# Twelve odd heads in rounded passes, their halves made during the attention

## What is computed

```python
x = x + attn(layernorm(x))        # elu(q)+1, elu(k)+1; kv = kp^T v; out = qp kv / (z + EPS)
x = x + xattn(ctx, ctx, layernorm(x), ssm_kernel, D, 8)
x = x + ffn(layernorm(x))         # 16 experts, top 4, and a shared expert

# xattn, for k = v = ctx (8, 256, 512), 32 heads of 8 channels, sequence 256:
kv = einsum('bhil,bhjl->bijhl', k_, v_)          # products of channel pairs
y = irfft(rfft(kv) * rfft(ssm_kernel))[..., :L]  # causal convolution for each head
out = einsum('bijhl,bhil->bjhl', y + kv * D, q_)
```

## Time and profile before

| | |
|---|---|
| median of 3 runs | 861.2 us (860.97 to 863.88) |
| the profiled execution | 860.96 us, span 859.1 us |
| TensorE busy | 840.3 us, 98% |
| DVE, ACT, POOL busy | 543.6, 378.1, 446.6 us |
| attention | 0 to about 243 us |
| heads 2 to 31 | 249 to 399 us |
| TensorE's granted clock, mean | 0.997 |

### The profile page before, as it was taken

How to read it: one execution, slowest core, us unless ns; L and a number is a source line. 1 busy time by engine, 2 the same in 40 slices (tenths; PEclk the granted TensorE clock), 3 DMA queues, 4 the chain that set the end, 5 groups by cost and what they waited for, 6 DMA issues and landing times.

```text
span 859.1 us, 14219 instructions
## 1 busy us (share of the span) xinstructions
PE 840.3 (98%) x4346; PEld 702.4 (82%) x4346; DVE 543.6 (63%) x849; ACT 378.1 (44%) x608; POOL 446.6 (52%) x439
## 2 busy tenths in 40 slices
PE   8999999999999999999999999999999999999995
PEld 7888888889877777778888778888888888888884
DVE  6767767775657777888769875544555544555431
ACT  5313322333133533442652255555555555655552
POOL 2123213331068899884622344666656666656644
PEclk9999999999999999999999999999999999999998
DMA  9611101100026543440210396988989888999866
GB/s 286 239 40 33 18 25 36 37 12 13 1 62 197 167 128 111 124 133 16 93 63 6 116 339 154 224 200 209 194 190 222 203 217 191 191 198 223 204 118 85
DMA packets 55108, 114.21 MB, mean 133 GB/s; under 512 B 10720, under 2 KB 14816, under 8 KB 54944
## 3 DMA queue, kind: packets, MB, share of 16 engines
q1 hardware_dynamic: 38048, 73.28, 27.3%
q0 software_dynamic: 17024, 40.48, 25.3%
HBM read 83.07 MB, written 30.67 MB: 132 GB/s over the span
## 4 chain that ended last, share of the span: by engine, by line
PE 88%; DVE 5%; issue 2%; POOL 1%; ACT 1%; DMA 1%; POOLq 0%; DVEq 0%; ACTq 0%
PE PS L206 20%; PE PS L208 20%; PE PS L207 19%; PE PS L217 17%; PE PS L1647 4%; PE PS L706 2%; PE PS L697 1%; PE PS L635 1%; PE PS L640 1%; PE PS L1584 1%; PE PS L1574 1%; PE PS L1614 1%; PE PS L1583 1%; PE PS L1566 1%; DMA QY<-stat_d 1%
## 5 line engine op out<-in xcount | busy, mean ns | idle before, releaser
L206 PE MATMUL PS<-QY_rounded,wh 128*128 128x512 f32 (+1 forms) x376 | 153.2, 407 | 0.0
L208 PE MATMUL PS<-QY_rounded,wl 128*128 128x512 f32 (+1 forms) x376 | 145.7, 387 | 0.0
L1362 POOL DMA_INDIRECT out_y<-QY,idy x72 | 114.5, 1590 | 44.9 <-ACT QY L1456 33.6
L207 PE MATMUL PS<-QY_rounded,wh 128*128 128x512 f32 (+1 forms) x312 | 120.0, 385 | 0.0
L1918 DVE TENSOR_TENSOR hTl<-hh,hTh 128x512 fp32r<-128x512 f32 (+1 forms) x39 | 27.5, 705 | 107.6 <-ACT hTh L1437 104.1
L1339 POOL DMA_INDIRECT xg<-xs_d,idx x64 | 76.8, 1200 | 28.8 <-issue 14.2
L208 PEld LDWEIGHTS PS<-QY_rounded,wl 128*128 128x128 f32 x376 | 70.6, 188 | 15.1
L217 PE MATMUL PS<-qER,Tz 128*128 128x288 f32 x320 | 81.1, 407 | 0.5 <-DVE QY L1064 0.4
L217 PE MATMUL PS<-prod,Tz 128*128 128x288 f32 x320 | 80.5, 406 | 0.2 <-DVE term L1047 0.2
L206 PEld LDWEIGHTS PS<-QY_rounded,wh 128*128 128x128 f32 x376 | 71.0, 189 | 11.1
L1456 ACT ACTIVATE QY<-PS,WPOS 128x512 f32<-128x512 f32 x76 | 52.4, 690 | 55.1 <-PE PS L208 45.2
(11 more groups left out here) (238 smaller groups left out, 1868.3 us busy)
## 6 DMA issues: line engine op xcount, KB each, us to landing
ws<-in_gu_w SPq DMA_DIRECT2D x38, 512.0 KB
ws<-in_dn_w SPq DMA_DIRECT2D x20, 512.0 KB, 5.6
C<-in_ctx SPq DMA_DIRECT2D x32, 256.0 KB, 2.7
Tz<-kpad_d SPq DMA_DIRECT2D x32, 256.0 KB, 3.3
xs_d<-xn SPq DMA_DIRECT2D x16, 256.0 KB, 2.0
out_y<-X SPq DMA_DIRECT2D x16, 256.0 KB
X<-in_x SPq DMA_DIRECT2D x1, 3072.0 KB, 17.5
xn<-in_xT SPq DMA_DIRECT2D x6, 512.0 KB, 3.4
```

What stands on the lines that cost most here:

```text
L206: pe.matmul(out_, lh, rh, start=first, stop=False)
L207: pe.matmul(out_, lh, rl, start=False, stop=False)
L208: return pe.matmul(out_, ll, rh, start=False, stop=last)
L1362: nc.gpsimd.indirect_dma_start(out=out, out_offset=bass.IndirectOffsetOnAxis(ap=idy[:, t:t + 1], axis=0), in_=yo[:, t], in_offset=None, co ...
```

## The change

Twelve odd heads (HALVES: 7, 9, ... 29) are convolved with three_pass, from halves of their products and of their Toeplitz rows. The Toeplitz halves are made once from kpad (POOL, into aTh and aTl) and stored in kpad_hl_d. The halves of the products are made during the attention, two heads in each of the batches 1 to 6: POOL makes the products into prod (in two parts and a small one), ACT rounds them into a free part of QY, POOL subtracts, and SP stores both to prod_hl_d. In the convolution stage SP loads them again, high and low part at different heads (load_half), into two sets of new buffers. The other twenty heads (WHOLE) stay as they were, but share the two product buffers in a new order, and the loops over heads are written out. mr, the spread statistics, moves from QY to Tz[0]. On DVE x_add comes before z_lo, att_norm(b) ends step b, and ln_norm(1, b-2) follows the next batch's statistics. Semaphores of the weight halves are merged into w_hi and w_lo; shared_lo comes in six parts in place of three.

```diff
+AHEAD = 2
+HALVES = [2 * m + 1 for m in range(3, 3 + AHEAD * (B - DIRECT))]
+WHOLE = [h for h in range(CH) if h not in HALVES]
...
+            def ahead_batch(b, last=False):
+                n = b * AHEAD - DIRECT * AHEAD
+                made = b * AHEAD_STEP - DIRECT * AHEAD_STEP
+                for j in range(AHEAD):
+                    sp.wait_ge(ahead_hi, n + (j + 1))
+                    store_half(0, n + j, ahead_high, hi_out)
+                    sp.wait_ge(ahead, made + AHEAD_MADE[j])
+                    if last:
+                        load_context(sp, WHOLE[j], j)
+                    else:
+                        ahead_context(n + AHEAD + j, j)
+                    sp.wait_ge(ahead, made + AHEAD_LOW[j])
+                    store_half(1, n + j, ahead_prod, lo_out)
...
+            def products_ahead(j, s):
+                pool.wait_ge(c2_in[j], s * 16 + 16)
+                wait_apart(pool, lo_out, s * (16 * AHEAD) + 16 * j)
...
+            def low_ahead(j, s):
+                wait_apart(pool, ahead_hi, s * AHEAD + j + 1)
+                nc.gpsimd.tensor_tensor(ahead_prod.bitcast(F32R), ahead_prod, ahead_high, ALU.subtract).then_inc(ahead, 1)
...
+            def high_ahead(b, j):
+                n = b - (DIRECT - 1)
+                wait_apart(act, ahead, n * AHEAD_STEP + AHEAD_MADE[j])
+                wait_apart(act, hi_out, n * (16 * AHEAD) + 16 * j)
+                act.activation(ahead_high.bitcast(F32R), ahead_prod, ACT.Copy).then_inc(ahead_hi, 1)
...
                 if not first:
+                    x_add(b - 1)
                     if not (last or isinstance(b, int) and b < DIRECT - 1):
                         z_lo(b + 1)
-                    x_add(b - 1)
                 kv_mask(b)
...
+                def load_half(n, j):
+                    k = n % 2
+                    if n < len(HALVES):
+                        t, dst = ((TzHi[k], odd_h[k]), (TzLo[k], odd_l[k]))[j]
+                        src = bass.AP(tensor=kpad_hl_d.tensor, offset=(j * CH + HALVES[n]) * (KPAD + 1), ap=[[1, P], [1, D]])
+                        sp.dma_start(t[:], src).then_inc(halves_in[k], 16)
+                        sp.dma_start(dst[:].rearrange("p c b n -> p (c b n)"), prod_hl_d[j, n]).then_inc(halves_in[k], 16)
...
+                def convolve_halves(h, behind=None):
+                    n, m = HALVES.index(h), h // 2
+                    k = n % 2
+                    pe.wait_ge(halves_in[k], 64 * (n // 2 + 1))
+                    pe.wait_ge(y_read[1], 2 * m)
+                    for c in range(DC):
+                        o = PS[:, DC + c].rearrange("p (b n) -> p b n", n=YGAP)[:, :, 0:NPAIR]
+                        for r in range(c + 1):
+                            w = slice((c - r) * P, (c - r + 1) * P)
+                            mm = three_pass(pe, o, TzHi[k][:, w].bitcast(F32R), TzLo[k][:, w].bitcast(F32R), odd_h[k][:, r].bitcast(F32R), odd_l[k][:, r].bitcast(F32R), r == 0, r == c)
```

More of the change, by code:

```diff
@@ L136, in decoder_program @@
         kpad_done, kpad_out = sem("kpad_done"), sem("kpad_out")
+        kpad_hl = [a[:].rearrange("p c s -> p (c s)")[0:CH, 0:KPAD + 1] for a in (aTh, aTl)]
+        ahead, ahead_hi = sem("ahead"), sem("ahead_hi")
+        hi_out, lo_out = sem("ahead_hi_out"), sem("ahead_lo_out")
+        halves_in = [sem(f"halves_in{k}") for k in range(2)]
+        NPROD = B * NPAIR
+        ahead_high = QY[:].rearrange("p c b s -> p c (b s)")[:, :, (B - 2) * S:(B - 2) * S + NPROD]
+        ahead_prod = prod[0][:].rearrange("p c b n -> p c (b n)")
+        AHEAD_MADE, AHEAD_LOW, AHEAD_STEP = (3, 7), (4, 8), 8
         tz_in = [sem(f"toeplitz_in{k}") for k in range(2)]
@@ L328, in _ @@
             pool.wait_ge(xns[1], TPB * B)
-            products(pool, 1, 0)
+            products(pool, 2)
         @block_.scalar
@@ L529, in step @@
             def step(b, first=False, last=False):
-                if not first:
-                    att_norm(b - 1)
                 if first:
@@ L565, in step @@
                     ln_stats(1, b - 1)
-                    if last:
-                        att_norm(b)
+                att_norm(b)
+                if last:
                     ln_norm(1, b - 1)
@@ L930, in _ @@
                     sp.dma_start(out[rows], zrow[:, 0:D]).then_inc(zero_out, 16)
-                with sp.Fori(3 + SLOT_T, normal_head(0) // 2) as i:
+                for i in range(3 + SLOT_T, normal_head(0) // 2):
                     next_heads(i)
@@ L963, in shared_lo @@
                                             ).then_inc(fixed_lo, 1)
-                with pool.Fori(2, 6) as i:
+                for i in range(2, 6):
                     pair_of_heads(i)
@@ L968, in _ @@
                 nc.gpsimd.tensor_tensor(gw_hl[:, :, 1], gw[:], gw_hl[:, :, 0].bitcast(F32), ALU.subtract).then_inc(fixed_lo, 1)
-                for part in range(NG - 1):
-                    pair_of_heads(6 + part)
-                    shared_lo(2 * part, 2 * part + 2)
+                for i in range(6, stream_head(0) // 2):
+                    pair_of_heads(i)
+                    shared_lo(i - 6, i - 5)
                 for i in range(stream_head(0) // 2, CH // 2):
-                    products(pool, i, 1)
                     for e in range(EARLY):
```

218 lines of the change are left out of this document (142 added, 76 removed).

## The result

The changed kernel took 867.46 us (median of 5, 864.09 to 869.2), the kernel before, in the same comparison, 860.97 us (860.58 to 863.88): a ratio of 1.0055 [1.0037, 1.0072], slower by 0.4 to 0.7% (the two medians alone would give 1.0075). Of all executions behind the numbers of this document two, one of e2 at 4885 us and one of e10 at 2971 us, stand far outside, and the ratios leave them out. The forecast was 856.0 us, in a range of 852.5 to 862.5. The profiled execution of the changed kernel took 864.09 us (span 861.8), the shortest of its five, 3.1 us over the profiled execution of before.

A forecast was written before the change was run, and what follows sets the result against it. TensorE, busy 840.3 of 859.1 us, was taken as the bound. 861.0 - 8.0 (heads) + 1.75 (swap) + 1.0 (batch 1) + 0.3 (late loads) gave 856.0 us; 8-in-10 range 852.5 to 862.5.

The forecast's parts named there:

- The heads: Convolution stage: twelve rounded heads gain 0.85 us each, 10.2 us, less 2.2 lost to DVE: 8.0 us gained.
- the pairs 20/21, 22/23 and 24/25: Heads with residual sum and statistics: DVE sets the pace at 10.46 us a pair, losing 2.2 us of the gain.
- Rival 5: Convolution heads: rounded passes paced by weight loads of 0.19 us, 5.7 us a head, 871 us; 2%.
- The hold in front of aTl: Attention: POOL's low half holds DVE's two sums to 131.4, aTl ends 134.0, before oproj at 134.23; no cost.
- ACT's copy: Attention batch: done by 12.3 us, just fitting the 4.01 us idle in front of kE; cost nothing.
- Rival 2: Attention: aTl late by 1.1 us in five batches, 5.5 us, so no change at 861 us; 25%.
- the swap: DVE, x_add before z_lo: KV's mask 0.35 us later in batches 2 to 6, 1.75 us lost.
- batch 1: Attention's first batch: POOL's second products beside z_lo cost 1.0 us, up to 1.4.
- Loads: First rounded heads: loads that come a little late, 0.3 us added.
- rival 4: Convolution stage: loads of halves too slow; at 200 GB/s a pair takes 11.1 us, total near 870 us; 6%.

The follow-up runs named there:

- e2: Changed kernel with halves made in batch 1 alone, ten rounded heads loading other heads' products: 877.74 us, total not comparable.
- e10: Changed kernel with only POOL's second products waiting for DVE's z_lo, low halves left whole: 857.71 us, ratio 0.9929 to the kernel before.
- e3: Changed kernel with all halves made and stored but never loaded, all 32 heads convolved in f32: 870.58 us, ratio 1.0120 to the kernel before.
- e7: e6 plus the shared expert's two weight loads and their rounding a pair of heads later: 853.5 us, ratio 0.9917 to the kernel before.
- e11: Changed kernel with only the shared expert's weight loads and their rounding a pair of heads later: 863.49 us, ratio 1.0003 to the kernel before.
- e6: Changed kernel with POOL's low half in four pieces and second products waiting for DVE's z_lo: 855.69 us, ratio 0.9936 to the kernel before.

## Why the prediction was wrong, step by step

- **The heads: the size right, the place partly luck.** The forecast had 8.0 us of gain. It is 8.0 (changed kernel against e3, without head 6's wait) and 8.1 (e7 against e3), from head 2 to the routing. But DVE was to set the pace in the pairs 20/21, 22/23 and 24/25, at 10.46 us. The pair 20/21 took 9.70 and gave its whole gain; 22/23, 24/25 and 26/27 took 10.44, 10.48 and 10.41, with TensorE waiting for DVE in head 23, 25 and 27 (0.33, 0.34, 0.77 us). DVE falls behind a pair later than I had it and hasn't caught up in 26/27. Three pairs either way, so the sum came out. Rival 5 did not come.
- **The hold in front of aTl, put at nothing: the step that failed.** The forecast priced POOL's low half on the two sums in front of aTl by the stretch in the rows (1.4 us for two instructions), found that aTl still ends in front of oproj, and had no term for it in the sum. In the runs DVE's instruction stands until POOL's has ended, and the next one stands again if POOL goes on with z: the two sums take 4.89 us instead of 1.29, or the minimum takes 3.26 instead of 0.75 and the sums 2.39. Either way TensorE waits 1.2 us for aTl and a batch is 1.5 us longer (1.1 in batch 5, where the minimum alone was held), in batch 3 of the changed kernel 1.40 in front of oproj's first matmul and 0.14 behind it. That was 5.7 us in four batches of the changed kernel and 7.6 in five of e11. Batches of 29 us or more with waits for aTl stood in the forecast as a sign that it is wrong.
- **Even the forecast's own times left no room.** It has the low half at 12.4 to 15.1 us of the batch, which is 131.6, and then reckons with 131.4. With 131.6 the sums end at 132.9 and aTl at 134.2, when oproj begins (134.23). "Still in front" was a matter of 0.2 us of reckoning.
- **What the forecast did not see.** It followed ACT's copy and asked whether it fits in front of kE's exponential. It fits: the copy ends at 103.79, the exponential begins at 104.12. POOL's low half starts when that copy ends, 12.41 us into the batch as forecast, right when DVE makes the input of ACT's next piece. The minimum 0.3 us ahead of it was not on the list, since I took "both inputs in SBUF" as the condition of the hold, from the one row that showed it (the earlier trace rows against the earlier trace rows). The minimum has one input, and was held in three of the changed kernel's batches.
- **Rival 2** had it: the place (aTl), the way (two sums held around a z instruction, as in e11 and in batch 6) and nearly the size (1.1 to 1.3 us late; the wait was 1.23). It was given 25%. Its 5.5 us for five batches were 7.6 in e11, so that even its 861 was low.
- **The attention's other terms.** Forecast 1.75 for the swap and 1.0 for batch 1. The swap costs under 0.1 (e6). Its price came from adding durations: three DVE instructions in a row of 0.69 us each start 0.60 us apart in e6 (139.89, 140.50, 141.10), and the mask begins at 141.70, not 141.94; before, it was 141.65. Batch 1 lost 1.2 us.
- **The size of POOL's stretch.** The rows of after and e10 show a wait to the end of POOL's instruction: the second half of the minimum ends at 106.93, POOL's at 106.64. The Trainium skill, page "SBUF — State Buffer", section "Who interferes with whom", says that the pair of ports goes to whoever issues first, for the whole instruction, and that tensor_scalar in its two-port mode wants it as well as instructions with two SBUF inputs. The trace agrees on both counts: 3.26 against 0.75 us for the minimum, 3.78 against 1.28 for the sums. That the minimum ran in that mode no run here shows. I had cited the rule for the second kind only, and set it aside for the smaller price.
- **Loads: 0.3 forecast, 2.0 measured,** all at head 6. The DMA engines were full around it (a share of 1.00 from 266 to 280 us), which the forecast had named as a sign of being wrong; rival 4 came for this one head. With the same share (0.99) but the 1 MB of weights behind them, the due rows came in time (e11): the order in the queue decided.
- **What stays open.** The traces explain 2.7 us of span between the two profiled executions; the medians differ by 6.5. The other four executions of the changed kernel have spans of 863.9 to 867.0 us at a mean granted clock of 0.990 to 0.992, the profiled one 861.8 at 0.993. No trace of the longer ones exists, so in which stage they lose isn't known. They need not be the change's doing: of the 22 executions of before that e10 and e11 were timed against, four have spans of 865.2 to 867.9 us, at a mean granted clock of 0.989 to 0.992, where the others have 858.4 to 861.6 at 0.993 to 0.997. How much of the 0.4 to 0.7% is of this kind isn't shown; the traces alone give 0.3%. Whether the split of e6 is worth anything over e10 isn't settled by the medians either (their intervals overlap).

## What to carry to other kernels

Before POOL work is put into a gap, list every DVE instruction that can run beside it, here also one with a single SBUF input. Price each that feeds the critical chain at the whole remaining length of the POOL instruction, and the one behind it at the next POOL instruction, not at a stretch. Where the times leave a few tenths of a microsecond, the place isn't settled: it changed from one execution to another (e10's batch 1, e11). Here 1.3 us of shift turned most of a loss of 8.5 us up to the last att into one of 1.1 (e10). So fix it with a wait on the DVE instruction that it must not meet, and look at the place again in the first batch, where nothing came before. And put a bulk load behind the small ones that are due first, in queue order.

## What the runs showed that I had not expected

- A DVE minimum with a single SBUF input (TENSOR_SCALAR, f32) was held by a POOL subtraction, 3.26 us for 0.75, and in e2 by z's instruction, 1.87.
- Two DVE sums were held by two POOL instructions in turn: 4.89 us for 1.29.
- Four POOL pieces of 288 elements take 3.98 to 4.50 us where one of 1152 takes 2.68; in batch 1 of e6 and e7, 3.11.
- The wait of 2.43 us in batch 1 was followed by a granted clock of 0.66 from 60 to 65 us, the wait of 2.55 us at the same place in e11 by 1.00 and an att of 2.07 us. So nearly the same pause was followed by a lower clock in one execution and not in another; a clock loss like this, seen in a single trace, isn't to be put on the kernel. In the changed kernel's trace it stood in for a hold: batch 2 lost 1.6 us either way, by the clock there, by the sums in e11.
- With DMA doing 145.89 MB instead of 114.21, a load of 256 KB of Toeplitz rows landed in 5.3 us instead of 3.3 (medians), and no head but one waited for a load.
